# The rotary part of a latent attention: cosine and sine parts of one head on one set of 128 rows

## The reference, cut to what matters

```python
q = (cq @ w_qb.T).reshape(b, s, H, DQ).transpose(0, 2, 1, 3)      # 16 heads, DQ = 128 + 64
q_nope, q_pe = (q[..., :DN], q[..., DN:])                         # DN = 128, DR = 64
q_pe = q_pe * cos + rotate_half(q_pe) * sin
k_pe = ckv[..., KVLR:].reshape(b, s, 1, DR).transpose(0, 2, 1, 3) # one for all heads
k_pe = k_pe * cos + rotate_half(k_pe) * sin
q_full = jnp.concatenate([q_nope, q_pe], axis=-1)
k_full = jnp.concatenate([k_nope, broadcast(k_pe)], axis=-1)
scores = jnp.einsum('bhqd,bhkd->bhqk', q_full, k_full) * scale
```

## Time and profile before

| what | value |
| --- | --- |
| median of three runs | 729.77 us |
| the profiled execution, device time | 731.32 us |
| its span, first to last instruction | 729.6 us |
| PE busy in the span | 710.9 us (97%) |
| DVE busy | 611.0 us (84%) |
| ACT busy | 435.0 us (60%) |
| mean granted clock of TensorE | 0.998 |

### The profile page before, as it was taken

How to read it: one execution, slowest core, us unless ns; L and a number is a source line. 1 busy time by engine, 2 the same in 40 slices (tenths; PEclk the granted TensorE clock), 3 DMA queues, 4 the chain that set the end, 5 groups by cost and what they waited for, 6 DMA issues and landing times.

```text
span 729.6 us, 16489 instructions
## 1 busy us (share of the span) xinstructions
PE 710.9 (97%) x6716; PEld 441.3 (60%) x6716; DVE 611.0 (84%) x942; ACT 435.0 (60%) x597; POOL 11.3 (2%) x36
## 2 busy tenths in 40 slices
PE   8999999999999999888999989999999999999998
PEld 3544444444444444445777758777777777777775
DVE  4778999999999998776888986788888888888885
ACT  4677777777777787834668844444444444444442
POOL 3000000000000000001000000000000000000000
PEclk9999999999999999999999999999999999999999
DMA  8560101010100010014242512577777777777770
GB/s 316 176 264 1 60 2 60 1 60 2 59 3 1 12 49 1 4 47 174 77 134 92 191 44 64 175 240 238 224 243 228 234 242 245 217 242 237 227 243 33
DMA packets 29864, 94.17 MB, mean 129 GB/s; under 512 B 5824, under 2 KB 15088, under 8 KB 28400
## 3 DMA queue, kind: packets, MB, share of 16 engines
q1 hardware_dynamic: 28944, 92.31, 38.6%
q10 hardware_dynamic: 864, 1.07, 0.5%
HBM read 92.76 MB, written 0.57 MB: 128 GB/s over the span
## 4 chain that ended last, share of the span: by engine, by line
PE 90%; DVE 3%; ACT 3%; DMA 2%; issue 1%; SPq 0%; POOL 0%; ACTq 0%; DVEq 0%
PE pS L1184 39%; PE pP L1184 29%; PE pO L1184 13%; PE pD L1184 9%; DMA arena<-in_wkT 1%; DMA mask_i<-in_mask 1%; ACT arena L540 1%; PE pO L1552 1%; DVE arena L781 0%; DVE arena L899 0%; DVE xn L1102 0%; ACT arena L593 0%; SPq L312 0%; ACT arena L578 0%; PE pS L1386 0%
## 5 line engine op out<-in xcount | busy, mean ns | idle before, releaser
L1184 PE MATMUL pS<-arena 128*128 128x256 f16 (+3 forms) x2185 | 254.2, 273 | 1.9 <-ACT arena L578 0.8
L1184 PEld LDWEIGHTS pS<-arena 128*128 128x128 f16 (+1 forms) x2185 | 213.5, 101 | 46.2 <-issue 2.1
L1184 PE MATMUL pP<-arena 128*128 128x512 f16 x980 | 239.4, 382 | 0.6 <-ACT arena L460 0.6
L1184 PEld LDWEIGHTS pP<-arena 128*128 128x128 f16 x980 | 91.9, 99 | 124.5 <-issue 12.2
L540 ACT ACTIVATE arena<-pS,mblk 128x1024 f32<-128x1024 f32 x128 | 147.3, 1205 | 8.8 <-PE pS L1184 8.8
L1013 DVE SCALAR_TENSOR_TENSOR arena<-arena 128x1536 f16<-128x1536 f32 x72 | 126.1, 1752 | 0.8 <-ACT arena L654 0.8
L694 ACT ACTIVATE arena<-pS 128x256 f32<-128x256 f32 x72 | 27.6, 383 | 154.2 <-PE pS L1184 154.2
L1184 PE MATMUL pO<-arena 128*32 128x256 f32 (+7 forms) x1370 | 108.6, 359 | 1.9 <-DVE arena L1008 1.9
L654 ACT ACTIVATE arena<-arena 128x1536 f16<-128x1536 f32 x72 | 106.4, 1477 | 1.0 <-PE pP L1184 1.0
L867 DVE TENSOR_SCALAR arena<-arena 128x1024 f32<-128x1024 f32 x128 | 87.1, 691 | 17.6 <-ACT arena L540 14.8
L1184 PE MATMUL pD<-arena 128*128 128x512 f16 x288 | 77.9, 379 | 0.0
(11 more groups left out here) (252 smaller groups left out, 493.5 us busy)
## 6 DMA issues: line engine op xcount, KB each, us to landing
arena<-in_units SPq DMA_DIRECT2D x72, 768.0 KB, 4.9
arena<-w_scratch SPq DMA_DIRECT2D x136, 64.0 KB, 2.7
arena<-in_ctxT SPq DMA_DIRECT2D x7, 1024.0 KB, 4.9
mw_in<-in_mla_in SPq DMA_DIRECT2D x8, 832.0 KB, 6.7
mw_out<-in_mla_out SPq DMA_DIRECT2D x8, 512.0 KB, 3.7
wlatT<-in_wlatT SPq DMA_DIRECT2D x1, 1280.0 KB, 10.6
arena<-in_ctxT ACTq DMA_DIRECT2D x4, 256.0 KB, 6.5
arena<-in_wkT SPq DMA_DIRECT2D x4, 256.0 KB, 5.6
```

Of the source, the lines that this page charges most:

```text
L1184: return pe.matmul(o, lhsT, rhs, start=start, stop=stop, **kw)
```

## The change

The layout of the rotary part is turned: one head's cosine part and sine part lie together on 128 partitions, and the two heads lie side by side in columns, where before the two heads shared the 128 partitions and the two parts lay in columns. For this `rope_mul` becomes four DVE instructions of 64 partitions by 256 columns, of which two read partitions of one half and write those of the other. The rotary products of a row block become 6 of 128 partitions instead of 12 of 64, with the heads in the outer loop. The keys are no longer doubled: `rotate_keys` writes 64 columns instead of 128, `turn_keys` makes one transpose per row block instead of two, and `kpeh`, `kpel` have 256 columns instead of 512. `rope_hi` and `rope_lo` keep their size.

```diff
--- before.py
+++ after.py
@@ -184,8 +184,8 @@
         xsum = take(TT)
         xmean = take(TT)
         xsq = take(TT)
-        kpn = take(TT * 4 * DR).rearrange("p (t i h d) -> p t i h d", t=TT, i=2, h=2)
-        kpeh, kpel = (take(2 * T, f16).rearrange("p (i t) -> p i t", i=2) for _ in range(2))
+        kpn = take(TT * 2 * DR).rearrange("p (t i d) -> p t i d", t=TT, i=2)
+        kpeh, kpel = (take(T, f16) for _ in range(2))
         qcs = take(2 * T).rearrange("p (i t) -> p i t", i=2)
         qnh, qnl, knh, knl = (take(4 * T, f16).rearrange("p (b j t) -> p b j t", b=2, j=2) for _ in range(4))
         vv = take(4 * T).rearrange("p (b t n) -> p b t n", b=2, t=TT)
@@ -220,7 +220,7 @@
         lat_raw = (pO[:, 0, :], pP[:, :])
         lat_t = (pD[:, :], pO[:, 0, :])
         kpe_ps = (pS[:, 2, 0:2 * DR], pS[:, 3, 0:2 * DR])
-        kpeT = pO[:, 1, :].rearrange("p (i t) -> p i t", i=2)
+        kpeT = pO[:, 1, 0:T]
         q_part, kv_part = slice(0, QC * QW), slice(QC * QW, QC * QW + 512)
         mx = take(4).rearrange("p (t j) -> p t j", t=2)
         nm = take(4).rearrange("p (t j) -> p t j", t=2)
@@ -953,8 +953,7 @@
                                                     cs_r[:, t, i].unsqueeze(1).broadcast_to([128, 2, DR]), ALU.mult, ALU.mult)
                 link(last)
                 for i, op in ((0, ALU.subtract), (1, ALU.add)):
-                    last = dve.tensor_tensor(kpn[:, t, i], kcos[:, t, i].unsqueeze(1).broadcast_to([128, 2, DR]),
-                                             ksin[:, t, 1 - i].unsqueeze(1).broadcast_to([128, 2, DR]), op)
+                    last = dve.tensor_tensor(kpn[:, t, i], kcos[:, t, i], ksin[:, t, 1 - i], op)
                 last.then_inc(s["kpn_ready"], 1)
 
             def add_eps(t):
@@ -991,8 +990,12 @@
 
             def rope_mul(m, p, at=None):
                 dve.wait_ge(s["mproj_done"], at if at else 4 * m + 2)
-                dve.scalar_tensor_tensor(qcs, pS[:, 1, 0:T].unsqueeze(1).broadcast_to([128, 2, T]), SH / (SA * SW), cs,
-                                         ALU.mult, ALU.mult).then_inc(s["rope_mul"], 1)
+                for i in range(2):
+                    for j in range(2):
+                        rows = slice(64 * j, 64 * j + 64)
+                        last = dve.scalar_tensor_tensor(qcs[64 * i:64 * i + 64, j], pS[rows, 1, 0:T], SH / (SA * SW),
+                                                        cs[rows, i], ALU.mult, ALU.mult)
+                last.then_inc(s["rope_mul"], 1)
 
             def rope_lo(m, p):
                 dve.wait_ge(s["rope_hi"], m + 1)
@@ -1407,9 +1410,7 @@
 
             def turn_keys(t):
                 pe.wait_ge(s["kpn_ready"], t + 1)
-                for i in range(2):
-                    last = pe.transpose(kpeT[:, i, 128 * t:128 * t + 128], kpn[:, t, i].rearrange("p h d -> p (h d)"), ident[:, :])
-                return last
+                return pe.transpose(kpeT[:, 128 * t:128 * t + 128], kpn[:, t].rearrange("p i d -> p (i d)"), ident[:, :])
 
             turn_rows(0)
             pe.wait_ge(s["wl_lo"], HC)
@@ -1517,12 +1518,10 @@
 
                 def rotary(t, lo, hi, start, stop):
 
-                    for k, (q, w) in enumerate(((qpeh, kpeh), (qpeh, kpel), (qpel, kpeh))):
-                        for i in range(2):
-                            for j in range(2):
-                                r = slice(64 * j, 64 * j + 64)
-                                last = mm(out_of(t, j, lo, hi), q[r, p, i, 128 * t:128 * t + 128], w[r, i, 0:hi - lo],
-                                          start and k == 0 and i == 0, stop and k == 2 and i == 1)
+                    for j in range(2):
+                        for k, (q, w) in enumerate(((qpeh, kpeh), (qpeh, kpel), (qpel, kpeh))):
+                            last = mm(out_of(t, j, lo, hi), q[:, p, j, 128 * t:128 * t + 128], w[:, 0:hi - lo],
+                                      start and k == 0, stop and k == 2)
                     return last
 
                 nope(0, 0, 128, True, False)
```

## The result

| | median us | runs from to | ratio to before, 95% |
|---|---|---|---|
| before | 729.90 | 729.39 to 730.89 (4) | |
| after | 737.54 | 736.21 to 738.77 (4) | 1.0103 (1.0078 to 1.0127) |

The change makes the kernel slower, by 5.7 to 9.3 us. The forecast was 735.7 with a range of 733.2 to 737.7. The profiled execution of after took 736.61 us with a span of 734.9, against 731.32 and 729.6 before: 5.3 us more, for which 5.9 were forecast.

What follows compares the result with a forecast made beforehand. PE's work and the way over `rope_mul`, `rope_hi` and L610 were taken to bind latent attention together. Prologue +0.87, pairs +0.79, +1.98, +2.37, -0.10 make +5.9 us: 735.7 on the 729.77 median, range 733.2 to 737.7.

Steps and rivals of the forecast that it cites:

- Two chains bind at once: Latent attention: PE's work and the way p_ready, `rope_mul`, `rope_hi`, L610, weighted sums bind within 0.13 us of each other.
- 0.21 us less in the scores of a pair: Scores on PE: 12 + 12 matmuls take 1.98 us against 2.19, counted in pairs 0 to 6.
- Four instructions that do not overlap, 1.00 us: `rope_mul` on DVE: 4 x 0.42 = 1.68 us, 1.00 more than 0.68; the forecast's middle case, chance 0.60.
- The rival of overlap: `rope_mul` on DVE: the four start 0.34 us apart, 0.76 more; +4.0 in all, 733.8 us; chance 0.22.
- The periods: Pairs of the latent attention, delay less scores gain: +0.79 us in pairs 0 and 4 to 6, +0.66 in 1 to 3.
- The last term: Pair 7: the second row block waits 0.40 us for ACT first, so only the change back is gained, -0.10 us.
- VectorE just fits: DVE's queue moves by about 1.1 us, leaving 0.14 us idle ahead of the mask in pair 2; DVE adds nothing.
- VectorE becomes the bound: Rival on DVE's queue: with 0.45 us or more per `rope_mul` instruction, +0.96 us, 736.7 us; chance 0.12.
- The prologue: Ahead of the first scores: `rope_mul` delay +1.00 us less 0.13 for the key rotation, +0.87.
- The key rotation: Prologue, L956: halved, 128 columns less, a gain of 0.13 us in row block 0.
- Not slower: Rival: the delay is absorbed on the way and the scores alone count, -1.7 us, 728.1 us; chance 0.06.
- The top of the range: Upper end of the forecast range: the case where DVE binds, with 1.0 us more, 737.7 us.

Runs made afterwards that it cites:

- The scores alone: The changed kernel with `rope_mul` as one instruction over 128 partitions again, against the kernel before: 729.74 us, ratio 0.9981.
- the four instructions alone: The kernel before with only `rope_mul` cut into four of 64 partitions by 256 columns, in two orders: 738.01 us (partitions change once), 738.91 us (each time).
- the swap on ACT: The changed kernel with the evacuation of the turned probabilities ahead of `rope_hi` on ACT: 735.72 us, ratio 1.0057 to the kernel before.
- the version that had lost 1.2 us: The changed kernel with four ACT copies moving the rows, one `rope_mul` product and some reordering: 732.16 us, ratio 1.0016 to the kernel before.

## Why the prediction was right, and where it was off

- **Two chains bind at once.** Right. The scores alone gave 0.20 to 0.22 us a pair, so TensorE's chain binds; the four instructions alone cost 0.69 and 0.89 us in each of pairs 1 to 3, so the one over `rope_mul` and L610 does too.
- **0.21 us less in the scores of a pair.** Right: 24 matmuls in 1.99 us, for 1.98 worked out. In pairs 4 to 6 too (11.24 to 11.02 with the scores alone).
- **Four instructions that do not overlap, 1.00 us.** Right in kind, a little low: `rope_mul` and `rope_hi` start 1.75 us apart in pair 2, against 0.71 in the earlier trace rows, 1.04 us more. The rival of overlap had 0.34 between starts; it was measured where partitions stay, and 0.42 to 0.44 where they change.
- **The periods.** Forecast 0.79, 0.66, 0.66, 0.66, 0.79, 0.79 and, for the last with `rope_mul` in it, 1.00; measured 0.82, 0.68, 0.68, 0.66, 0.83, 0.82, 1.04. The 0.04 us of the line above is in nearly each. The last term, in pair 7 (its second row block), was -0.10 for -0.10.
- **VectorE just fits.** Right: 0.09 us left for 0.14 forecast. How near the rival "VectorE becomes the bound" was, the swap on ACT shows: VectorE's queue binds 0.18 us further down. In after it does not bind: a mask that starts 0.60 us behind L1055 would, here they are 0.77 apart.
- **The prologue.** The key rotation gave 0.14 us and `rope_hi` came 0.90 later, as forecast (0.87). The step that was mis-sized is what follows it: from `rope_hi` to the first mask before took 5.20 us and after 5.88, +0.68, where the gain of the scores was to make it -0.21. Two terms were missing. The first is 0.12 us: `lo_q` (L1006) starts 0.72 us behind `rope_lo` (L1002) for 0.61, when that is done (342.76 + 0.69 = 343.45). Its input in PSUM starts at partition 0, and the last instruction that read PSUM was the fourth L996, from partition 64; `rope_lo` between them reads none. By the rule of the Trainium skill, "VectorE: DVE Perf Modes", section "Two Vector instructions with no wait between them", quoted above, it is held for this. The traces agree: with one `rope_mul` from partition 0 (the change on TensorE alone) the two start 0.61 us apart, and 0.72 in after and in both kernels of the four instructions alone, whose last one also reads from partition 64. The rows with one `rope_mul`, against those of after in the section on the result:

```profile
344.35 0.69 DVE L998 TENSOR_TENSOR arena<-arena 128x512 f16<-128x512 f32 x1 [0.70 <-ACT arena L626]
344.96 0.68 DVE L1002 SCALAR_TENSOR_TENSOR arena<-pS,arena 128x512 f16<-128x512 f32 x1
```

The forecast had looked for `lo_q` held right behind `rope_mul` only. The second is 0.77 us: TensorE's clock fell to 0.5 in the first scores, behind 3.06 us of idle time. The forecast added the delay to the wait and took the scores behind it at the full clock. How much of this term is due to the change is open, since the clock did not fall in every kernel with the same wait. Where it did not, with the swap on ACT, `rope_hi` to the first mask took 5.11 us, which is 5.20 + 0.12 - 0.21: the first term and the gain, and nothing else.
- **Not slower.** Wrong, as forecast: nothing absorbed the delay.

So the forecast was 1.1 us low for the latent attention (5.9 for 7.0): 0.9 from the way to the end of the first scores, of which 0.77 are the clock, and 0.2 from the 0.04 us. With the clock at 1.0 it would have been 0.3 us low. Against the median it was 1.8 us low; the 0.7 us that stay are less than the runs of after differ by (2.6 us). The median of 737.54 is within the range by 0.2 us, and two of the four executions, 738.47 and 738.77, lie above it. The top of the range was there for a VectorE that becomes the bound, which did not happen; that it also had room for the lower clock is luck.

## What to carry to other kernels

Where one engine is busy all the time, look at how late the others come before believing that it alone binds: here a change that took 0.2 us from TensorE put 1.0 us into a chain with 0.13 us of room. Ask what stands in order behind a late instruction without needing it; here the evacuation of the probabilities behind `rope_hi`, and with it taken from there, together with two moves around `rope_lo`, the version that had lost 1.2 us won 1.9. A wait of TensorE that gets longer is to be priced for itself, and the range is to have room for a lower clock behind it: it cost 0.77 us here in the trace of after, and did not come each time. Before work is moved to GpSimd, look at what VectorE does at that time: of two instructions that met here, the second stood until the first was done.

## What the runs showed of the hardware

- VectorE: products of 256 columns start 0.34 us apart on the same partitions and 0.42 to 0.44 apart on changing ones. A 512-column product of 0.68 us cut into four of half the partitions and half the columns takes 1.52 to 1.73 us.
- ACT: four copies of 64 partitions and 256 columns between PSUM and SBUF take 1.54 us, 0.385 us each, one behind the other.
- GpSimd beside VectorE: a 128x1024 TENSOR_TENSOR on GpSimd (2.1 to 2.3 us) and a VectorE product of 1152 columns (1.35 us), both with all operands in SBUF, take turns. In the twelve pairs of two kernels in which they overlapped, the first to start kept its time, and the second ended 1.21 to 1.22 us behind it if it was VectorE's and 1.99 to 2.00 us if it was GpSimd's. The TENSOR_SCALAR of the same size (2.77 us) left the VectorE TENSOR_TENSOR of 512 columns (`rope_lo`) beside it, also all in SBUF, at 0.68 us; but a VectorE TENSOR_SCALAR of 128x2 beside it took 1.02 us, for 0.17 in before (pair 7).
- TensorE's clock: the stretches at 0.5 (1.2 GHz) in before and after were 3.4 us long each, and 256-column matmuls started 0.213 us apart in that of after, for 0.109 at 1.0. The one in after's first scores came behind 3.06 us of idle time; behind 3.07 and 3.06 us in two other kernels there was none. The one around 329 us in before follows waits of 1.73 and 0.78 us; after has the same two, 1.74 and 0.78, and a clock of 1.0. So it is in all twelve kept traces: the same two waits, and a stretch at 0.5 behind them in six. The rows of PE there, of before and then of after:

```profile
326.48 0.66 PE L1386 MATMUL pS<-ident,xn 128*128 128x128 f32 x4 [1.73 <-DVE xn L933]
327.91 1.01 PE L1184 MATMUL pS<-arena 128*128 128x128 f16 x8 [0.78 <-ACT arena L578]
```

```profile
326.16 0.65 PE L1389 MATMUL pS<-ident,xn 128*128 128x128 f32 x4 [1.74 <-DVE xn L933]
327.60 0.61 PE L1187 MATMUL pS<-arena 128*128 128x128 f16 x8 [0.78 <-ACT arena L578]
```

The same eight matmuls take 1.01 us in the one and 0.61 in the other. What decides it there is open.
